# Row maxima of a causal attention as a stream of their own, and float32r score products in pairs of row halves

## The chip, the cores and the metric

The kernel runs on one core of a Trainium2 chip. The metric is device time in microseconds (us) for one execution; the number given is the median of several runs. Five engines of the core work side by side and wait for each other through semaphores: TensorE (PE in the profile; PEld is its weight load), VectorE (DVE), ScalarE (ACT), GpSimd (POOL) and SyncE (SP), which here only issues DMAs. TensorE writes its products to PSUM, eight banks of 128 partitions by 512 float32; everything else lies in SBUF or in DRAM.

## What is computed

The input `x` is 4 sequences of 1024 tokens with 256 features. After a layer norm, one branch is a causal attention with 16 heads of 16 features, the other a feed-forward chain of six blocks (256 to 1024 to 256, exact GELU), and the two are joined with a SiLU gate.

```python
def attention(x, w_qkv, w_out):
    q, k, v = split(x @ w_qkv)                       # (4, 1024, 16 heads, 16)
    scores = einsum('bqhd,bkhd->bhqk', q / 4, k)
    scores = where(causal_mask, scores, -1e10)
    attn = softmax(scores, axis=-1)
    return einsum('bhqk,bkhd->bqhd', attn, v).reshape(b, s, 256) @ w_out

def ffn(x, W1, B1, W2, B2, LN_G, LN_B):
    for i in range(6):
        h = gelu(x @ W1[i].T + B1[i])                # 1024 hidden, exact gelu
        x = h @ W2[i].T + B2[i] + x
        if i < 5:
            x = layernorm(x, LN_G[i], LN_B[i])
    return x

xn = layernorm(x)
out = x + attention(xn, w_qkv, w_out) * silu(ffn(xn, ...))
```

## The kernel before

Four stages follow each other, each a block with a program of its own for every engine, and a barrier between two.

**Projection** (`project`). The 4096 tokens come in 8 groups of 512 (`GROUPS`, `GT`). A group is normalised, transposed, split into a high float32r part and a low rest (`p_gth`, `p_gtl`) and multiplied with the weights, split in the same way: three products (high by high, high by low, low by high) stand for one of full precision. Queries and keys are split into three bfloat16 parts and stored in DRAM (`q_parts`, `k_parts`). The transposed input is kept in SBUF for all tokens (`xth`, `xtl`), and so are its rows (`xres`).

**Feed-forward** (`mlp`). A *slot* is one block applied to one group of 512 tokens; there are 48. A slot has 8 *chunks* of 128 hidden units. For chunk k TensorE does `up(k)` (line 752: six products of 512 columns into `m_h_ps`), then `down(k - 2)` (line 763: twelve products of 256 columns into `m_y_ps`). ACT computes the GELU twice (lines 626 and 628, in float32 and rounded to float32r), DVE takes the difference (line 687, `m_hidl`), and both parts feed `down`. Before each slot of the blocks after the first, eight transposes (line 785) make the transposed input anew. In each slot DVE also adds the residual (line 663), computes statistics (lines 694 and 704) and both halves of the layer norm (lines 711 and 722), and splits one piece of the next block's weights (lines 651 to 655). `sweep` runs the slots in hardware loops. In the last two slots the row maxima of attention group 0 are searched beside the chunks (`piece`, `piece_max`). The rows go to DRAM (`mlp_out`).

**Attention** (`attend`). A *group* is 4 heads of one sequence, 16 in all. A softmax needs the maximum of each row of scores. So the scores are computed twice: first with the queries on the partitions, in 38 *pieces* of up to 512 columns per group (`piece_products`, lines 114 and 117; the second one adds the causal mask as a product with the identity), of which DVE takes the maximum (`row_max`, line 129). The negated maxima, in three bfloat16 parts, are transposed, and become three rows more of the query stack (rows 96 to 98; the key stack has ones there). Then the scores are computed with the keys on the partitions (line 1153, 99 rows deep, `a_st_ps`), ACT takes the exponential (line 1003, `a_prob`), POOL clears what lies above the diagonal (line 977), and TensorE multiplies with the values, four heads side by side on 32 columns each of its array (line 1172, `a_o_ps`). The *stacks* `qs` and `ks` of a group hold the parts in 96 rows; SP loads them with 12 DMAs of 16 rows each (`load_stacks`, line 99), two groups ahead, into one of four buffers. TensorE's order within a group comes from a plan computed while the program is written: `pace` counts columns and puts the pieces of the next groups where, by the constants `DVE_COLUMN`, `ACT_COLUMN` and so on, their bank is free. ACT also copies the results (line 1014). At the end SP first issues four loads for the last stage (`load_pair`), then the store of the last group.

**Combination** (`combine`). Tile by tile of 128 tokens the attention output is divided by its row sums, multiplied with `w_out`, gated with SiLU, added to `x` and stored.

## Time and profile before

| | us |
|---|---|
| median of 3 runs | 1801.35 |
| the runs | 1800.85 to 1807.49 |
| span of the profiled execution | 1806.1 |
| TensorE busy, share of that span | 95% |
| DVE busy | 64% |
| ACT busy | 53% |
| POOL busy | 18% |

The span is that of one profiled execution, 4.75 us above the median. Its stages, by the times at which their first and last products stand in the trace: projection until 95.3 us, feed-forward from 106.4 to 1239.7 us, attention until 1719.8 us, combination from 1741.8 us to the end. A matmul's row in the trace lasts longer than the time it keeps the array, since products overlap; the distance from one start to the next is what a product costs. So a busy share near 100% says that TensorE had something in flight, not that it worked at its best.

### The profile page before, as it was taken

How to read it: one execution, taken by the hardware profiler on the slowest of the kernel's cores; microseconds unless marked ns; L12 is line 12 of the kernel's file. 1: busy time of each engine (PE TensorE's matmuls, PEld its weight loads, DVE VectorE, ACT ScalarE, POOL GpSimd, SP SyncE). 2: the span in 40 equal slices, each digit the busy share in tenths (PEclk: the TensorE clock that was granted, in tenths of full speed). 3: DMA queues.
4: the chain of work that ended last, by engine and by line, in shares of the span. 5: the costliest groups of instructions: out<-in, count | busy, mean ns of one | idle time of the engine just before them, and what ended most of it. 6: DMA issues, size and time to landing. Idle time of an engine off the chain costs nothing. (4 is left out here: it accounts for less than half of the span.)

```text
span 1806.1 us, 33624 instructions
## 1 busy us (share of the span) xinstructions
PE 1716.2 (95%) x11664; PEld 1312.9 (73%) x11664; DVE 1149.1 (64%) x2325; ACT 958.0 (53%) x1364; POOL 323.2 (18%) x317
## 2 busy tenths in 40 slices
PE   6979999999999999999999999997999989999947
PEld 5869999999999989999999998875444433444236
DVE  7846666666666656666666643366877866877326
ACT  5834555555555545555555554432666665666723
POOL 3511111111111111111111111110121211121214
PEclk9989999999999999999999999998999998999969
DMA  6940000000000000000000050003474754574113
GB/s 206 306 140 13 12 17 16 13 12 17 13 9 12 17 16 12 13 17 12 16 12 12 0 83 24 23 24 64 76 112 75 109 84 73 88 107 73 48 57 137
DMA packets 104427, 97.97 MB, mean 54 GB/s; under 512 B 26636, under 2 KB 88588, under 8 KB 104316
## 3 DMA queue, kind: packets, MB, share of 16 engines
q1 hardware_dynamic: 104256, 96.39, 23.9%
q8 instruction: 69, 1.13, 0.3%
q14 instruction: 42, 0.34, 0.1%
q10 hardware_dynamic: 60, 0.10, 0.0%
HBM read 62.15 MB, written 29.62 MB: 51 GB/s over the span
## 5 line engine op out<-in xcount | busy, mean ns | idle before, releaser
L626 ACT ACTIVATE m_hid<-m_h_ps,m_b1s 128x512 f32<-128x512 f32 x384 | 264.3, 688 | 571.0 <-PE m_h_ps L752 558.9
L687 DVE TENSOR_TENSOR m_hidl<-m_hid,m_hidh 128x512 fp32r<-128x512 f32 x384 | 307.4, 809 | 323.9 <-ACT m_hidh L628 322.8
L129 DVE TENSOR_REDUCE mx<-a_s_ps 128x1 f32<-128x512 f32 (+3 forms) x570 | 341.2, 656 | 91.3 <-PE a_s_ps L117 87.8
L1003 ACT ACTIVATE a_prob<-a_st_ps 128x1024 f32<-128x1024 f32 (+1 forms) x320 | 289.9, 938 | 168.5 <-PE a_st_ps L1153 123.0
L752 PE MATMUL m_h_ps<-xth,shared 128*128 (+1 forms) x768 | 269.8, 397 | 12.3 <-DVE shared L655 12.2
L763 PE MATMUL m_y_ps<-shared,m_hidh 128*128 128x256 f32 x1536 | 277.9, 281 | 0.0
L628 ACT ACTIVATE m_hidh<-m_h_ps,m_b1s 128x512 fp32r<-128x512 f32 x384 | 261.8, 682 | 0.0
L763 PEld LDWEIGHTS m_y_ps<-shared,m_hidh 128*128 128x128 f32 x1536 | 246.6, 189 | 12.0 <-DVE m_hidl L687 0.4
L602 POOL TENSOR_TENSOR y<-y,m_b2s 128x1024 f32<-128x1024 f32 x47 | 112.8, 2400 | 708.3 <-DVE y L663 708.3
L763 PE MATMUL m_y_ps<-m_w2h,m_hidh 128*128 128x256 f32 x768 | 217.9, 284 | 0.6 <-DVE m_hidl L687 0.3
L763 PE MATMUL m_y_ps<-shared,m_hidl 128*128 128x256 f32 x768 | 215.8, 281 | 0.0
L763 PE MATMUL m_y_ps<-m_w2h,m_hidl 128*128 128x256 f32 x768 | 215.5, 281 | 0.0
L763 PE MATMUL m_y_ps<-m_w2l,m_hidh 128*128 128x256 f32 x768 | 215.4, 280 | 0.0
L752 PEld LDWEIGHTS m_h_ps<-xth,shared 128*128 128x128 f32 x768 | 145.3, 189 | 39.9 <-DVE shared L655 12.9
L1172 PE MATMUL a_o_ps<-a_prob,a_va 128*32 128x512 f32 (+3 forms) x1536 | 165.9, 504 | 1.4 <-issue 1.3
L752 PE MATMUL m_h_ps<-xth,m_w1h 128*128 (+1 forms) x384 | 155.5, 405 | 2.5 <-issue 2.5
L752 PE MATMUL m_h_ps<-xtl,shared 128*128 (+1 forms) x384 | 152.0, 396 | 0.0
L752 PE MATMUL m_h_ps<-xtl,m_w1h 128*128 (+1 forms) x384 | 151.7, 395 | 0.0
L763 PEld LDWEIGHTS m_y_ps<-m_w2h,m_hidh 128*128 128x128 f32 x768 | 144.3, 188 | 8.9 <-issue 2.3
L763 PEld LDWEIGHTS m_y_ps<-m_w2l,m_hidh 128*128 128x128 f32 x768 | 146.6, 191 | 5.0
L752 PE MATMUL m_h_ps<-xth,m_w1l 128*128 (+1 forms) x384 | 150.1, 391 | 0.1
L977 POOL TENSOR_SCALAR_AFFINE_SELECT a_prob<-a_prob 128x512 f32<-128x512 f32 x128 | 81.5, 637 | 379.6 <-ACT a_prob L1003 379.0
(115 smaller groups left out, 2648.3 us busy)
## 6 DMA issues: line engine op xcount, KB each, us to landing
q_parts<-p_part SPq DMA_DIRECT2D x16, 384.0 KB, 3.5
k_parts<-p_part SPq DMA_DIRECT2D x16, 384.0 KB, 3.0
m_raw<-w1t SPq DMA_DIRECT2D x48, 128.0 KB, 2.2
m_raw<-w2t SPq DMA_DIRECT2D x48, 128.0 KB, 2.4
shared<-q_parts SPq DMA_DIRECT2D x48, 128.0 KB, 4.6
shared<-k_parts SPq DMA_DIRECT2D x48, 128.0 KB, 7.7
a_qs<-q_parts SPq DMA_DIRECT2D x48, 128.0 KB, 4.6
a_ks<-k_parts SPq DMA_DIRECT2D x48, 128.0 KB, 7.4
```

The costliest lines, as they stand in the source:

```text
L129: return nc.vector.reduce_max(mx[:, half, first:first + heads, qt], scores, AX_X)
L602: nc.gpsimd.tensor_tensor(y[yu][:], y[yu][:], b2s[epar][:].broadcast_to([P, TILES, DIM]), ALU.add).then_inc(b2_added, 1)
L626: nc.scalar.activation(hid[k % 2][:], h_ps[k % 2][:], ACT.Gelu, bias=b1s[s.par][:, k:k + 1])
L628: nc.scalar.activation(hidh[k % 4][:], h_ps[k % 2][:], ACT.Gelu, bias=b1s[s.par][:, k:k + 1]).then_inc(gelu_done, 1)
L687: nc.vector.tensor_tensor(hidl[k % 4][:], hid[k % 2][:], hidh[k % 4][:].bitcast(F32), ALU.subtract).then_inc(low_done, 1)
L752: i = nc.tensor.matmul(h_ps[k % 2][:], w[s.par][:, c, k * P:(k + 1) * P], x[:, c, tokens], start=(c == 0 and w is w1h and x is xth), stop= ...
L763: i = nc.tensor.matmul(y_ps[s.u][:, j, :], h[k % 4][:, j * P:(j + 1) * P], w[s.par][:, k, :], start=(k == 0 and j % 2 == 0 and h is hidh a ...
L977: nc.gpsimd.affine_select(out=diag, in_=diag, compare_op=ALU.is_ge, fill=0.0, base=0, pattern=[[0, HG], [1, P]], channel_multiplier=-1).th ...
L1003: nc.scalar.activation(prob[step % BUFS][:, j:j + heads, 0:hi - lo], unit_ps(unit), ACT.Exp).then_inc(exp_done, 1)
L1172: i = nc.tensor.matmul(o_ps[2 * HD * j:2 * HD * (j + 1), lo - BANK * half:BANK], va[u][:, kt, j, :], prob[step % BUFS][:, j, 0:hi - lo], s ...
```

## The change

The search for row maxima becomes a class of its own, `MaxSearch`, with a list of 336 *visits*: 20 pieces and one transposition for each of 16 groups. The first 209 visits, that is groups 0 to 9 but for the last transposition, lie in the feed-forward stage; 127 lie in the attention stage, over its first 14 groups, about one for each step of a group. A visit writes into one pair of banks, `s_ps`, and has to wait until DVE is through with the visit before.

Queries and keys are split into two float32r parts instead of three bfloat16 ones. A stack then has 48 rows (three products of parts by 16), or 50 with the two parts of the shift. Two heads lie on the rows 0 to 63 and two on 64 to 127 (`SIDE`), so that two products, one of each side, use different row halves of TensorE's array. This holds for the search (`pe_visit`) and for the scores. The causal mask of the search leaves TensorE: DVE adds it from SBUF and takes the maximum with one `tensor_tensor_reduce` for each head, on the pieces that touch the diagonal; the others are one reduction of 1024 columns. Stacks for attention have two buffers instead of four; those of the search have two more (`mq`, `mk`), and so each group's parts are loaded twice. The shifts go through DRAM (`shifts`).

In the feed-forward stage the rows stay in SBUF in place (`xres`), the transposed input is kept for two slots only, all 48 slots transpose, the scaling with the norm's weights goes to POOL, the normalisation to ACT, and `m_y_ps` has one buffer instead of two. The first block's weights are split during the projection. `xtl` and `mlp_out` are no longer stored. In attention a group has 10 steps and 18 exponentials, all of 1024 columns, instead of 12 steps and 20; DVE copies the results instead of ACT. All loops but those of `combine` are written out.

```diff
-PARTS = 3
-STACK = 6 * HD
+PARTS = 2
+STACK = 3 * HD
 ROWS = STACK + PARTS
...
+SIDE = P // 2
+PAIR = 2
+AHEAD = 10
...
+    def pe_visit(s, pe, s_ps, v):
...
+        for c in range(columns):
+            for side in range(2):
+                if c == 0 and v:
+                    pe.wait_ge(s.maxed, 2 * v - 1 + side)
+                rows = slice(SIDE * side, SIDE * side + STACK)
+                i = s.nc.tensor.matmul(s_ps[:, side, c * keys:(c + 1) * keys], s.q[m % 2][rows, first + c, qt * P:(qt + 1) * P],
+                                       s.k[m % 2][rows, first + c, half * BANK:half * BANK + keys], start=True, stop=True)
+        i.then_inc(s.done, 1)
...
+        if qt // HG != half:
+            s.nc.vector.reduce_max(mx[:, half, first::PAIR, qt], s_ps[:, :, 0:keys], AX_X).then_inc(s.maxed, 2)
+        else:
+            for side in range(2):
+                for c in range(columns):
+                    h = PAIR * side + first + c
+                    i = s.nc.vector.tensor_tensor_reduce(s.unused[:, v % 2, side, c * keys:(c + 1) * keys], s_ps[:, side, c * keys:(c + 1) * keys],
+                                                         s.causal[:, BANK - keys:BANK], 1.0, NEG, ALU.add, ALU.max, mx[:, half, h:h + 1, qt])
+                i.then_inc(s.maxed, 1)
...
+        for v in range(VISITS):
+            slot, place = divmod(2 * v, 9)
+            AT.setdefault(CH * (1 + slot) + (1, 4, 4, 5, 5, 6, 6, 7, 7)[place], []).append(v)
...
+            turn(0)
+            for n in range(CHUNKS + 2):
+                if n < CHUNKS:
+                    up(n)
+                if n % CH == 2 and n // CH + 1 < SLOTS:
+                    turn(n // CH + 1)
+                if n >= 2:
+                    down(n - 2)
+                for v in AT.get(n, ()):
+                    search.pe_visit(pe, s_ps, v)
...
+                    if n and n + 1 < N_GROUPS:
+                        sp.wait_ge(st_done, NU * n)
+                        load_stacks(sp, scratch, qs[(n + 1) % 2], ks[(n + 1) % 2], n + 1, keep["qk_loaded"][(n + 1) % 2])
+                        sp.wait_ge(search.stored, 16 * (n + 2))
+                        load_shift(sp, scratch, qs[(n + 1) % 2], n + 1, keep["qk_loaded"][(n + 1) % 2])
...
+            for at in range(ALL + LATE + 1):
+                n, step = divmod(at, NS)
+                if at < ALL:
+                    scores(n, FIRST_OF[step])
+                if 0 <= at - LATE < ALL:
+                    values(at - LATE)
+                if at < ALL and LAST_OF[step] > FIRST_OF[step]:
+                    scores(n, LAST_OF[step])
+                for v in AT.get(at, ()):
+                    search.pe_visit(pe, s_ps, v)
```

TensorE in the feed-forward stage, at the seam of two chunks. Before, `down` (line 763) is followed by `up` (line 752) directly:

```order
L763 MATMUL m_y_ps<-m_w2h,m_hidh 128x256
L763 MATMUL m_y_ps<-m_w2l,m_hidh 128x256
L763 MATMUL m_y_ps<-m_w2h,m_hidl 128x256
L749 REGISTER_ALU
L752 MATMUL m_h_ps<-xth,m_w1h 128x512
L752 MATMUL m_h_ps<-xtl,m_w1h 128x512
L752 MATMUL m_h_ps<-xth,m_w1l 128x512
```

Now, in four or five chunks of each slot, a pair of search products of line 164 stands between them (`mk`, `mq` are the search's stacks):

```order
L686 MATMUL m_y_ps<-w2h,m_hidh 128x256
L686 MATMUL m_y_ps<-w2l,m_hidh 128x256
L686 MATMUL m_y_ps<-w2h,m_hidl 128x256
L164 MATMUL m_s_ps<-mk,mq 128x512 x2
L673 MATMUL m_h_ps<-m_xth,w1h 128x512
L673 MATMUL m_h_ps<-m_xtl,w1h 128x512
L673 MATMUL m_h_ps<-m_xth,w1l 128x512
```

What moved in is a block of another shape of the array between two full ones.

TensorE in attention, before: pieces of the search (lines 114 and 117), scores (line 1153) and values (line 1172) in the plan's order.

```order
L1153 MATMUL a_st_ps<-shared 128x384
L1172 MATMUL a_o_ps<-a_prob,a_va 32x512 x4
L1151 REGISTER_ALU
L1153 MATMUL a_st_ps<-shared 128x384 x2
L1151 REGISTER_ALU
L1153 MATMUL a_st_ps<-shared 128x256 x4
L1165 REGISTER_ALU
L1172 MATMUL a_o_ps<-a_prob,a_va 32x512 x4
```

Now: scores are line 878, values line 897, the search line 164.

```order
L878 MATMUL a_st_ps<-shared 128x512 x2
L164 MATMUL a_s_ps<-mk,mq 128x512 x2
L878 MATMUL a_st_ps<-shared 128x512 x2
L897 MATMUL a_o_ps<-a_prob,va 32x512 x4
L878 MATMUL a_st_ps<-shared 128x512 x2
L164 MATMUL a_s_ps<-mk,mq 128x512 x2
```

A step has two pairs of scores, one block of values and one visit; the order no longer depends on a plan of when banks come free.

SP in attention, now: the loads of a group's stacks (line 86, `shared`) and shift (line 93), a search load (line 86, `mq` and `mk`) after the results' store, and then the next group's stacks.

```order
L782 DMA x_rows<-x 128x2x256
L86 DMA shared<-q_parts 16x2x1024 x6
L86 DMA shared<-k_parts 16x2x1024 x6
L93 DMA shared<-shifts 2x2048 x2
L105 DMA v_raw<-values 128x8x64
L775 DMA attention_t<-a_oout 17x1024 x4
L86 DMA mq<-q_parts 16x2x1024 x6
L86 DMA mk<-k_parts 16x2x1024 x6
L782 DMA x_rows<-x 128x2x256
L86 DMA shared<-q_parts 16x2x1024 x6
```

The stacks of group n + 1 are now loaded while group n runs; before they were loaded two groups ahead. The search loads, four in this stage, stand in the same queue.

## Rows read from the trace of the kernel before

**Rows 1.** Busy time by stretch: us, PE, PEld, DVE, ACT, POOL, PEclk, DMA share, GB/s

```profile
0.00:95.30 95.30, 79.43 (x448) 68.15 (x448) 71.46 (x146) 65.58 (x96) 45.51 (x50) 1.00 0.77 258
95.30:106.40 11.10, 0.02 (x1) 0.02 (x1) 1.26 (x4) 2.33 (x3) 1.62 (x2) 0.59 0.58 184
106.40:1239.70 1133.30, 1126.54 (x7312) 1015.84 (x7312) 681.78 (x1377) 561.54 (x848) 160.20 (x87) 1.00 0.08 19
1239.70:1257.50 17.80, 8.77 (x38) 4.28 (x39) 11.11 (x21) 1.30 (x2) 2.58 (x4) 0.62 0.57 110
1257.50:1719.80 462.30, 452.97 (x3483) 180.36 (x3481) 339.27 (x648) 302.93 (x352) 89.86 (x143) 0.98 0.51 85
1719.80:1741.80 22.00, 0.00 (x0) 0.00 (x0) 1.12 (x2) 2.10 (x3) 0.00 (x0) 0.55 0.11 39
1741.80:1806.10 64.30, 48.46 (x384) 44.23 (x384) 43.10 (x128) 22.21 (x64) 23.42 (x32) 0.87 0.34 118
```

**Rows 2.** Timeline of TensorE in feed-forward: start us, us, line, operation

```profile
158.01 1.03 PE L785 MATMUL m_tr_ps<-ident,y 128*128 128x128 f32 x8
158.80 0.48 PE L752 MATMUL m_h_ps<-xth,shared 128*128 x1
...
700.68 0.40 PE L752 MATMUL m_h_ps<-xth,m_w1h 128*128 128x512 f32 x1
...
702.07 0.28 PE L763 MATMUL m_y_ps<-m_w2h,m_hidh 128*128 128x256 f32 x1
...
703.48 0.40 PE L752 MATMUL m_h_ps<-xth,m_w1h 128*128 128x512 f32 x1
```

**Rows 3.** Timeline of TensorE in attention: scores, a block of values, search pieces

```profile
1361.20 0.38 PE L1153 MATMUL a_st_ps<-a_qs,a_ks 99*128 99x512 bf16 x1
1361.51 1.06 PE L1172 MATMUL a_o_ps<-a_prob,a_va 128*32 128x512 f32 x8
1362.51 0.28 PE L114 MATMUL a_s_ps<-shared 96*128 96x256 bf16 x1
...
1366.08 0.38 PE L114 MATMUL a_s_ps<-shared 96*128 96x512 bf16 x1
1366.30 0.22 PE L117 MATMUL a_s_ps<-maskb,identb 128*128 128x128 bf16 x1
1366.36 0.76 PE L1153 MATMUL a_st_ps<-a_qs,a_ks 99*128 99x512 bf16 x3
```

**Rows 4.** Groups by line and shape: count | busy us, mean ns | idle before, releaser

```profile
L687 DVE TENSOR_TENSOR m_hidl<-m_hid,m_hidh 128x512 fp32r<-128x512 f32 x384 | 307.4, 809 | 323.9 <-ACT m_hidh L628 322.8
L626 ACT ACTIVATE m_hid<-m_h_ps,m_b1s 128x512 f32<-128x512 f32 x384 | 264.3, 688 | 571.0 <-PE m_h_ps L752 558.9 <-issue 3.5 <-DVE m_hidl L687 1.9
L129 DVE TENSOR_REDUCE mx<-a_s_ps 128x1 f32<-128x512 f32 x360 | 224.4, 683 | 62.3 <-PE a_s_ps L117 58.8 <-PE a_s_ps L114 3.3
L663 DVE TENSOR_TENSOR y<-m_y_ps,xres 128x1024 f32<-128x1024 f32 x48 | 58.8, 1225 | 111.1 <-PE m_y_ps L763 111.1
L704 DVE BATCH_NORM_AGGREGATE m_mv<-m_stats 128x2 f32<-128x6 f32 x160 | 14.8, 155 | 0.0
```

**Rows 5.** Timeline of the last attention group, which has no search beside it

```profile
1710.49 1.07 PE L1172 MATMUL a_o_ps<-a_prob,a_va 128*32 128x512 f32 x8
...
1712.13 3.69 ACT L1003 ACTIVATE a_prob<-a_st_ps 128x1024 f32<-128x1024 f32 x4 [0.34 <-PE a_st_ps L1153]
1712.45 1.07 PE L1172 MATMUL a_o_ps<-a_prob,a_va 128*32 128x512 f32 x8
```

**Rows 6.** Busy time by stretch again: stack loads alone, and the projection's middle

```profile
1042.00:1066.00 24.00, 24.00 (x161) 21.93 (x160) 13.61 (x27) 12.02 (x18) 3.59 (x2) 1.00 0.91 126
...
45.00:90.00 45.00, 43.49 (x261) 37.58 (x260) 37.55 (x68) 37.57 (x56) 25.81 (x23) 1.00 0.91 305
```

**Rows 7.** Timeline of SP's DMA issues, for one stack and at attention's end

```profile
1339.34 2.78 SPq L99 DMA_DIRECT2D shared<-q_parts  x6
...
1706.39 14.00 SPq L1195 DMA_DIRECT2D ot<-attention_t  x4
```

More of the change, by code:

```diff
@@ L121, in by_head @@
-def by_head(bank, piece):
-    _, _, _, heads, keys = piece
-    return bank[:, 0:heads * keys].rearrange("p (h n) -> p h n", n=keys)
-def row_max(nc, mx, scores, piece):
-    qt, half, first, heads, _ = piece
-    return nc.vector.reduce_max(mx[:, half, first:first + heads, qt], scores, AX_X)
-def project(nc, x, wqkv, scratch, keep):
+            columns = min(BANK // keys, PAIR)
+            pieces += [(qt, half, c, columns, keys) for c in range(0, PAIR, columns)]
+    return pieces
+PIECES = max_pieces()
@@ L591, in _ @@
+            for n in range(2):
+                sp.wait_ge(keep["qk_loaded"][n], (LOADS + NM_LOADS) * 16)
+            sp.wait_ge(keep["ones_loaded"], 4 * 16)
         @block.gpsimd
         def _(pool):
[L593 to L598 removed]
@@ L637, in _, with high, normalise @@
-            sweep(act, slot, begin)
+            def high(t):
+                act.wait_ge(transposed, t + 1)
+                nc.scalar.activation(xth[t % 2][:], tr_ps[:], ACT.Copy).then_inc(xth_done, 1)
+            def normalise(t):
+                act.wait_ge(shift_ready, t + 1)
+                for j in range(TILES):
+                    row = xres[:, TILES * (t % GROUPS) + j, :]
+                    m = nc.scalar.activation(row, row, ACT.Identity, bias=shift[:, j:j + 1], scale=rstd[:, j:j + 1])
+                m.then_inc(normed, 1)
@@ new lines, with attend @@
+DIAGONALS = [[sum(hi - lo for _, lo, hi in parts[:i]) for i, (kt, _, _) in enumerate(parts) if kt // HG == half] for half, parts in STEPS]
+SELECTS = sum(len(d) for d in DIAGONALS)
+BUFS = 3
+LATE = 2
+def attend(nc, x, wout, scratch, keep, search):
+    od = scratch["o"]
+    ALL = NS * N_GROUPS
+    VISITS = range(search.at[AHEAD, 0], len(search.visits))
+    AT = {}
+    weights = [0.5 if WIDTH[step] < BANK else 1.0 for step in range(NS)]
+    total = sum(weights) * (N_GROUPS - 2)
+    for v in VISITS:
+        due = total * (v - VISITS[0]) / len(VISITS)
+        at = 0
+        while due >= weights[at % NS]:
+            due -= weights[at % NS]
+            at += 1
+        AT.setdefault(at, []).append(v)
+    STEP_OF = {v: at for at, visits in AT.items() for v in visits}
```

1349 lines of the change are left out of this document (549 added, 800 removed).

## The prediction, made blind

> **What bounds the kernel now.** I read the busy time by stretch first, cut at the seams of the stages [rows 1]. The feed-forward stage takes 1133.3 us and has TensorE busy for 1126.5 of them at the full granted clock; attention takes 462.3 us with TensorE busy for 453.0. DVE and ACT are busy for 60% and 50% of the first, 73% and 66% of the second. Then the timeline, because a busy TensorE may still be slow. In feed-forward one chunk goes from 700.68 to 703.48: 2.80 us, of which `up` takes 1.39 and `down` 1.41 [rows 2]. 384 chunks are 1075 us, nearly the whole stage, so nothing but TensorE's products bounds it. In attention a block of values of 512 columns keeps TensorE for 1.00 us (1361.51 to 1362.51), a search piece of 512 columns with its mask for 0.28 us, and a score product for about 0.22 us [rows 3]. Per group (sums over the 36 tiles of 128 by 128 of a head): search 22528 columns, 9.9 us at 0.28 us per 640; scores 18432 columns, 7.9 us; values nine times 512 columns, 9.0 us, and about 0.25 us for each of 12 blocks that the array needs to change its shape. That is near 29 us, and a group lasts 465 / 16 = 29 us. TensorE bounds attention too, by the search above all.
>
> **Feed-forward.** Chunks stay as they are: 1075 us. Transpositions: 47 beside the first, where there were 40, each 0.79 us plus about 0.08 for the late product behind it [rows 2]: 41 us. New are 209 visits. The trace has no product on half the rows. The stream of a visit is 461 columns on average per half (9216 by 20 pieces), 0.21 us at the pace of `up`, if both halves run side by side; 0.42 if they don't. Changing the shape: around a block of values TensorE loses 0.09 us ahead (1361.20 plus 0.22 against 1361.51) and 0.15 us behind (1.00 against 0.85, which four times 512 columns take at 2.4 GHz) [rows 3], 0.24 in all. For a visit I add 0.10 for the second half's weights, which in a lone pair have nothing to hide behind. So 0.55 us each, 115 us in all. Bounds: 0.31 (no change of shape to pay), 65 us; 0.87 (halves in sequence, and float32r weights of 0.19 us uncovered twice), 182 us. I take 0.55, since the block of values is the nearest row.
>
> Do the others keep up? A visit costs DVE 1.22 us where it is one reduction of 1024 columns (the residual's row has this size) [rows 4]. On the diagonal it is two to four passes of together 512 to 1024 columns plus a read-out for each; the trace has no such instruction. At 0.68 us per 512 [rows 4] and 0.15 for the read-out (the short instruction of line 704), a mean visit costs 1.42 us; if the operation needed two passes, 2.0. Per slot DVE then has 6.5 (eight times 0.81), 1.2 for the transposed rest, 1.3 for the residual, 2.2 for statistics, 1.4 for weights and 6.4 for visits: 19 of 25 us. A visit waits for DVE's maximum of the one before, a chunk earlier; DVE starts about 2.3 us behind `up` and ends by 3.9, TensorE comes back at 4.7. No stall, while DVE has 0.8 us to spare. ACT loses a copy and gains four small ones; its two GELUs of 0.69 us leave half the chunk free [rows 4]. POOL gets two passes more for each slot, behind which nothing of the chunk waits. Stage: 1075 + 41 + 115 + 2 for the cold start = 1233 us against 1133.
>
> **Projection and its seam.** TensorE's work is the same. A group's DMA grows from 3.0 to 3.3 MB; in the middle of the stage the queues moved 305 GB/s at a share of 0.91 [rows 6], so up to 5 us may come on top. I take 97 us, and 10 for the seam (barrier, then a transposition in place of the wait for the first weights): 107 against 106.4.
>
> **Seam to attention.** Before 17.8 us [rows 1]: store of the rows, barrier, and a serial chain from the maxima of group 0 to the first exponential. The first two groups' stacks and shifts now land before. Residual 1.3, POOL 2.4, barrier 3, exponentials' table and first scores 2.3: 9 us.
>
> **Attention.** A group is 18 exponentials of 1024 columns. Back to back they start every 0.92 us (3.69 for four, with the last one's full length) [rows 5], so ACT needs 16.6 us per group and a full step, two of them, 1.84 us. TensorE in a full step: two pairs of scores 0.47, a block of values 1.00 and the change of shape 0.10, a visit next to the scores 0.23: 1.80 us. Both are nearly equal, and both wait for each other through two pairs of banks. The last group before the change, free of search but with scores of 0.88, ran at 1.96 us per full step (1710.49 to 1712.45) [rows 5]. I take 2.0. In addition a visit returns to DVE once a step: product 0.4, two passes with read-out 1.7, and TensorE is back after 2.0, so diagonal visits cost a few tenths. 19.5 us per group with search (14), 18.3 without (2): 310 us. Then DMA. A stack is 1.5 MB; 24 loads of 3 MB took 24 us at 126 GB/s and a share of 0.91 [rows 6], so one stack takes 12 us behind 5.6 us of issue time, half of it exposed [rows 7]. From the start of group n to the arrival of stack and shift for n + 1 I count 15 us of 19.5: hidden. Four search loads of 12 us stand ahead of a following stack in the same queue; they leave the next one about 3 us late each: 12 us. Start and tail 3 us. Together 325 us against 462.3.
>
> **The rest.** The results' last store still follows four loads of 14 us at SP [rows 7]; 22 us of seam and 64 us of combination stay [rows 1].
>
> **Sum.** 107 + 1233 + 9 + 325 + 22 + 64 = 1760 us, against the span of 1806.1. The median is 0.9974 of that span, so 1755 us. Attention and its seam give 146 us, feed-forward takes back 100. It is a difference of two large numbers, and both hang on the price of a pair on row halves.
>
> **Rival 1, slower: the two row halves don't run side by side.** A pair of 512 columns then costs 0.46 instead of 0.23 us. Feed-forward: 209 times 0.21, 44 us more. Attention: a full step has 0.93 + 1.10 + 0.46 = 2.5 us of TensorE, 23.2 us per group with search, 18.7 without: 365 us, 40 more. Span 1844, time 1839. It decides from the point at which a pair costs over 0.36 us, where the 46 us gained are gone. Against it: values of four heads, eight products of 512 columns, take 1.00 us on column strips [rows 3]; one after the other, at 0.22 us each, they would take 1.76. For it: no row shows row halves. The Trainium skill (TensorE: Matmul & The Clock Gate, Part 3) gives a speedup of 3.07 for four row tiles instead of 4; by that rate a pair would cost 0.30 us, and the forecast would move up by about 26 us. No row here has row tiles.
>
> **Rival 2: stack loads bound attention.** Rows are now 4 KB at a distance of 32 KB in DRAM, where they were 2 KB at 24 KB. If the rate fell from 126 to 90 GB/s, a stack would take 17 us, the chain 20.7 us per group, and each search load 13 us: 379 us for attention, time 1809. For it: attention's queues are at a share of 0.51 before, at a group time of 29 us [rows 1], which is 15 us of a group and leaves little of 19. Against it: the mean does not show that larger rows are slower. The Trainium skill (DMA: Bandwidth & Descriptors, in its table of pitfalls) warns of row pitches at large powers of two, 207 GB/s at 512 KB and less from 2 MB on; that alone is above the 126 GB/s measured here, and would change nothing.
>
> **Rival 3: the small prices vanish.** If the change of shape hides (0.31 us per visit) and ACT runs at 0.92 us throughout (266 us plus 17 for start and DMA), feed-forward is 1183 and attention 283: span 1668, time 1664.
>
> **How the numbers follow.** Forecast 1755 us, chance 0.66; in it lie the dearer DVE pass (attention 28 us more) and the dearer stores (5). Rival 3 has 0.10, rival 2 0.09, rival 1 0.15. The main case by itself reaches from 1700 to 1800. The range for 8 in 10 is 1685 to 1812: it takes in rival 2 and leaves out rival 1 and most of rival 3. Faster by over 0.5% (which is about what a measurement of this kernel can tell from no change): 0.66, less 0.03 for its upper end, plus 0.10, plus 0.03 of rival 2, so 0.76. Within 0.5%: 0.07. Slower: 0.17.
>
> **What would show it.** In the changed profile: chunks without a visit still 2.80 us apart, those with one 3.35; starts of the two products of a pair under 0.15 us apart, and the next full product about 0.5 us behind. Attention of about 19 to 20 us per group, with ACT's idle time under 15% and released by scores. In rival 1 the second product of a pair starts 0.2 us behind the first and ACT waits for TensorE a quarter of the time; in rival 2 TensorE's longest waits, once a group, end with a DMA into the stacks. DVE below 80% in feed-forward. I am wrong at the root if chunks without a visit grow, since that would mean a wait on DVE or ACT which I count as hidden.

## The result and the profile after

The changed kernel takes 1851.6 us (median of 4 runs, 1850.5 to 1853.8) against 1802.3 in the same comparison: a ratio of 1.027 (95% interval 1.025 to 1.029). It is slower by 49 us, where I had forecast 1755 and a gain of 46. The profiled execution has a span of 1848.7 us. Its stages, cut at the same seams as [rows 1] (the columns are those of [rows 1]); the fifth stretch is attention up to its last values, the sixth the seam and the combination's start:

```profile
0.00:112.90 112.90, 86.34 (x448) 73.78 (x448) 67.44 (x178) 35.78 (x48) 10.57 (x20) 0.92 0.70 240
112.90:122.20 9.30, 2.12 (x11) 1.58 (x9) 1.23 (x1) 3.33 (x3) 0.00 (x0) 0.63 0.52 152
122.20:1395.00 1272.80, 1250.14 (x7777) 1076.68 (x7777) 887.65 (x1842) 607.03 (x975) 378.55 (x169) 0.99 0.17 29
1395.00:1399.90 4.90, 1.40 (x10) 1.19 (x8) 0.86 (x2) 1.28 (x1) 2.34 (x1) 0.87 0.14 16
1399.90:1763.90 364.00, 313.48 (x2595) 128.08 (x2593) 169.29 (x491) 276.73 (x288) 87.20 (x142) 0.91 0.70 116
1765.00:1787.00 22.00, 1.17 (x8) 0.97 (x8) 1.59 (x4) 2.01 (x3) 0.00 (x0) 0.55 0.09 34
```

Against the terms of the sum: projection and its seam 122.2 (forecast 107), feed-forward 1272.8 (1233), seam 4.9 (9), attention 364.0 (325), the rest 84.8 (86). The differences are 15, 40, -4, 39 and -1 and make up the 89 us between the forecast span of 1760 and 1848.7. In three stages TensorE is no longer busy all the time: it is idle for 27 us of the projection (16 before), 23 of feed-forward (7) and 51 of attention (9).

The pair on row halves is not the cause. Timeline of TensorE in feed-forward (columns as in [rows 2]); `m_s_ps` is a visit of twice 512 columns:

```profile
699.93 0.50 PE L164 MATMUL m_s_ps<-mk,mq 48*128 48x512 f32 x2
700.36 0.50 PE L673 MATMUL m_h_ps<-m_xth,shared 128*128 128x512 f32 x1
...
703.36 0.50 PE L164 MATMUL m_s_ps<-mk,mq 48*128 48x512 f32 x2
703.79 0.50 PE L673 MATMUL m_h_ps<-m_xth,shared 128*128 128x512 f32 x1
```

Both products of the pair together last 0.50 us and the next product starts 0.43 behind the first; the first full product then needs 0.10 more than usual before the next one. In the trace the two products of such a pair start 0.003 us apart (median of 120 pairs of 512 columns), which is the sign that the prediction asked for. The chunk lasts 3.43 us. One without a visit lasts 2.82, against the 2.80 of [rows 2]: 0.02 more in each of 384 chunks is 8 us, and no wait.

### The profile page after: what moved, and what is told of

Read it like the earlier page. It is cut to its first block and busy times, and to the rows that moved or that the text cites. A ratio compares the mean times of both kernels' runs of the same rounds, so it can differ in the third digit from the quotient of the medians.

```text
span 1848.7 us, 29436 instructions
## 1 busy us (share of the span) xinstructions
PE 1700.0 (92%) x11216; PEld 1323.2 (72%) x11216; DVE 1171.2 (63%) x2644; ACT 947.8 (51%) x1380; POOL 502.0 (27%) x364
## 5 line engine op out<-in xcount | busy, mean ns | idle before, releaser
L840 ACT ACTIVATE a_prob<-a_st_ps 128x1024 f32<-128x1024 f32 x288 | 276.7, 1025 | 84.9 <-PE a_st_ps L878 82.5
L673 PE MATMUL m_h_ps<-m_xth,shared 128*128 128x512 f32 x768 | 285.9, 413 | 11.7 <-issue 9.3
L686 PE MATMUL m_y_ps<-w2h,m_hidh 128*128 128x256 f32 x768 | 217.2, 283 | 0.0
L686 PE MATMUL m_y_ps<-w2l,m_hidh 128*128 128x256 f32 x768 | 214.6, 279 | 0.0
L686 PE MATMUL m_y_ps<-w2h,m_hidl 128*128 128x256 f32 x768 | 214.1, 279 | 0.0
L897 PE MATMUL a_o_ps<-a_prob,va 128*32 128x512 f32 (+3 forms) x1536 | 167.5, 526 | 43.0 <-POOL a_prob L821 43.0
L673 PE MATMUL m_h_ps<-m_xth,w1h 128*128 128x512 f32 x384 | 163.4, 426 | 13.4 <-issue 13.4
L673 PE MATMUL m_h_ps<-m_xtl,shared 128*128 128x512 f32 x384 | 153.1, 399 | 0.0
L673 PE MATMUL m_h_ps<-m_xth,w1l 128*128 128x512 f32 x384 | 152.9, 398 | 0.0
L673 PE MATMUL m_h_ps<-m_xtl,w1h 128*128 128x512 f32 x384 | 152.3, 397 | 0.0
```

What stands on the lines that cost most here:

```text
L673: m = nc.tensor.matmul(h_ps[n % 2][:], w[i % 2][:, c, k * P:(k + 1) * P], x[t % 2][:, c, :], start=(c == 0 and w is w1h and x is xth), sto ...
L686: m = nc.tensor.matmul(y_ps[:, j, :], h[n % 4][:, j * P:(j + 1) * P], w[par][:, k, :], start=(k == 0 and j % 2 == 0 and h is hidh and w is ...
L840: nc.scalar.activation(to, scores, ACT.Exp).then_inc(exp_done, 1)
L897: i = nc.tensor.matmul(o_ps[half][2 * HD * j:2 * HD * (j + 1), lo - BANK * half:hi - BANK * half], va[n % 2][:, kt, j, :], prob[at % BUFS] ...
```

## Experiments

Each kernel is the changed one with the edits shown, unless it says otherwise, and a gain is against its 1851.6 us. Ratios are to the kernel before, timed beside it.

### 1 and 2. Five waits in feed-forward

The waits of TensorE on weights in this stage (who waited for whom: total us, times, longest) and, below, the timeline of all engines at one of them, the end of a block:

```profile
PE m_h_ps L673 <- issue: 22.7, 5, 4.8
```

```profile
539.12 2.39 POOL L553 TENSOR_TENSOR xres<-xres,m_lng 128x1024 f32<-128x1024 f32 x1 [6.85 <-ACT xres L572]
...
540.52 1.54 DVE L636 TENSOR_TENSOR m_hidl<-m_hid,m_hidh 128x512 fp32r<-128x512 f32 x1 [1.49 <-ACT m_hidh L587]
541.59 2.67 POOL L555 TENSOR_TENSOR xres<-xres,m_lnb 128x1024 f32<-128x1024 f32 x1
541.98 2.42 DVE L218 CAST shared<-raw 128x256 fp32r<-128x256 f32 x1
...
545.50 0.77 PE L673 MATMUL m_h_ps<-m_xth,shared 128*128 128x512 f32 x1 [4.80 <-issue]
...
546.07 0.63 PE L673 MATMUL m_h_ps<-m_xtl,shared 128*128 128x512 f32 x1
...
546.49 0.63 PE L673 MATMUL m_h_ps<-m_xth,shared 128*128 128x512 f32 x1
```

The reader is to see three things. DVE's difference `m_hidl` takes 1.54 us instead of 0.69 and the cast 2.42 instead of 0.29, both while POOL's passes for gain and bias run; the second pass ends at 544.26 and the cast at 544.40. The last split of the block ends at 545.40, and only then may the first `up` of the next block run, 4.80 us late. And behind the wait products of 512 columns start at a distance of 0.42 us instead of 0.23 (546.07 and 546.49): the clock has fallen to the lower level, 1.2 GHz (the granted clock is 1.00 from 540 to 545 us and 0.66 from 545 to 550), and the wait is paid a second time in part.

Experiment 1 moves the split to chunk 2:

```diff
-                if k == 7 and t < LAST:
+                if k == 2 and t < LAST:
                     dve.wait_ge(raw_loaded[g % 2], 32 * (t // 2 + 1))
                     split_piece(nc, dve, keep, (i + 1) % 2, g, w_high, t + 1).then_inc(w_split, 1)
```

> The changed kernel with one edit: DVE splits the slot's weight piece at chunk 2 instead of chunk 7. In the changed kernel feed-forward lasts 1272.8 us, and TensorE is idle for 22.7 us of it in five waits of up to 4.8 us, one ahead of the first `up` of each new block, which waits for the last of the eight splits. At chunk 7 POOL's two passes of 2.4 and 2.7 us run, and DVE's casts of the weights take 2.4 us and 1.8 us where the same shape took 0.29 us in the projection. Theory A (DVE's casts are held up by POOL's passes, and the split, ready only at the edge of the block, comes too late): the five waits go, with them some 4 us of lower clock behind them; feed-forward 1246 us, time 1825 (ratio 0.986 to the changed kernel's 1851.6, 1.013 to the one before). The casts fall to about 0.3 us, unless POOL's first pass meets them. Theory B (the wait at the edge has another cause, say x_ready behind POOL's longer chain or the transposed input): the waits stay, 1850.

Measured: 1830.1 us, ratio to before 1.015 (1.013 to 1.017), a gain of 21.5. The five waits are gone and the casts take 0.27 us (median). One new wait of 8.5 us came in the first slot, where the raw weights land 13.9 us after DVE asks for them, behind the first search loads; without it the gain would have been 30, against the 27 forecast. Feed-forward takes 1251 us instead of 1273.

Experiment 2 leaves the split where it was and takes POOL's two passes away:

```diff
-                    nc.gpsimd.tensor_tensor(xx, xx, lng[i % 2][:].broadcast_to([P, TILES, DIM]), ALU.mult).then_inc(scaled, 1)
-                    pool.wait_ge(scaled, t + 1)
-                    nc.gpsimd.tensor_tensor(xx, xx, lnb[i % 2][:].broadcast_to([P, TILES, DIM]), ALU.add).then_inc(x_ready, 1)
+                    nc.gpsimd.memset(idle[:], 0.0).then_inc(x_ready, 1)
```

> The changed kernel without the layer norm's gain and bias: POOL's two passes per slot (2.4 and 2.7 us) are replaced by a memset of one column, and the split stays at chunk 7. Left out of the computation: the scaling by gain and the bias in the feed-forward chain. Theory A (POOL's passes hold up DVE): the cast of the first weight takes 0.3 us instead of 2.4, the difference `m_hidl` about 0.81 us instead of 0.90, and the five idle waits of TensorE (22.7 us) vanish although the split stays where it is; time near 1825. Rival (DVE is simply behind at chunk 7, because of its visits at chunks 4 to 7): casts 0.3 us, but the waits stay at 2 to 5 us each, time 1840 to 1850. Rival (the raw weights land late): casts stay long, 1850.

Measured: 1828.3 us in one run. The groups of DVE in feed-forward, the changed kernel first, then this one (columns as in [rows 4]):

```profile
L636 DVE TENSOR_TENSOR m_hidl<-m_hid,m_hidh 128x512 fp32r<-128x512 f32 x384 | 346.3, 902 | 351.2 <-ACT m_hidh L587 350.4
L218 DVE CAST w1h<-raw 128x256 fp32r<-128x256 f32 x24 | 57.7, 2405 | 0.0
```

```profile
L635 DVE TENSOR_TENSOR m_hidl<-m_hid,m_hidh 128x512 fp32r<-128x512 f32 x384 | 283.9, 739 | 414.6 <-ACT m_hidh L586 414.4
L218 DVE CAST w1h<-raw 128x256 fp32r<-128x256 f32 x24 | 6.8, 285 | 0.6 <-DMA raw<-w2t 0.6
```

The cast falls from 2405 to 285 ns and the difference from 902 to 739, although nothing of DVE's own work was changed: POOL's passes hold up the cast and the difference, which read and write SBUF alone. The changed kernel's trace says so directly, too. 39 of its 40 first casts of this stage run beside the pass for the bias, take 2.5 us and end 0.15 us behind it (medians). The difference takes 0.69 us in 299 cases without a pass beside it and 1.55 in the 40 beside the pass for the gain (medians). What is left above 0.69 in the 739 comes from a third pass of POOL (line 546), which this run keeps. That agrees with the Trainium skill (SBUF — State Buffer, Who interferes with whom, with the rule it rests on in "SBUF: two separate sides"), by which a GpSimd instruction and a DVE instruction in a two-port mode, or one with two SBUF inputs if GpSimd's reads SBUF as well, exclude each other for their whole length. It also agrees that the reductions, which read PSUM, take 1.22 us, the ten wholly beside a pass of POOL as well as the other 70. Of the waits 7.8 us remained (five, up to 1.8), so the rival has a part: DVE is late at chunk 7 without these two passes, too.

### 3. The input's place in SP's queue

In the projection DVE waits 27.9 us, in 6 waits, for the group's input, since its load stands behind the stores of four parts, the values and two weight pieces.

```diff
-                if g + 2 < GROUPS:
-                    sp.wait_ge(normed, g + 1)
-                    load_x(g + 2)
+                if g == 0:
+                    sp.wait_ge(normed, 1)
+                    load_x(2)
                 for m in range(4):
+                    if m == 2 and g + 3 < GROUPS:
+                        sp.wait_ge(normed, g + 2)
+                        load_x(g + 3)
                     sp.wait_ge(part1_done, 4 * g + m + 1)
```

> The changed kernel with one edit in the projection: SP issues the load of a group's input one group earlier, between the query and the key stores, instead of behind the stores, the values and two weight pieces. In the changed kernel DVE waits 27.9 us in 6 waits for this input, and the stage ends at 112.9 us instead of 95.3. Theory A (the place in SP's queue): these waits go, the stage ends at 100 us or before, time 1839. Theory B (bytes: each group moves 3.3 MB instead of 3.0, and the queues' rate bounds the stage): input comes earlier but stores and weight pieces later; the stage ends at 110 or later, time 1848 to 1852.

Measured: 1829.8 us, ratio 1.015 (1.013 to 1.017), a gain of 21.8, more than theory A asked for. The middle of the stage (columns as in [rows 6]), the changed kernel first, then this one:

```profile
20.00:80.00 60.00, 49.76 (x272) 42.75 (x271) 36.73 (x102) 21.61 (x29) 5.03 (x5) 0.91 0.73 245
```

```profile
20.00:80.00 60.00, 60.00 (x364) 53.25 (x364) 51.31 (x137) 29.52 (x40) 6.05 (x6) 1.00 0.98 343
```

TensorE is busy throughout, at the full clock, and the queues move 343 GB/s at a share of 0.98. The first `up` starts at 99.7 us instead of 122.2, and 22 of these 22.5 us reach the end. So bytes did not limit the stage; they come close to it now.

### 4 to 7. The loads of the attention stage

In attention these waits of the changed kernel are the longest but for those of idle engines (waited for: total us, times, longest):

```profile
POOL va L111 <- DMA v_raw<-values: 139.3, 12, 18.8
...
ACT a_prob L840 <- PE a_st_ps L878: 82.5, 82, 12.1
...
PE a_o_ps L897 <- POOL a_prob L821: 43.0, 12, 10.4
```

and one group of them, from the timelines of SP, POOL and TensorE, in this order:

```profile
1470.47 0.38 SPq L105 DMA_DIRECT2D v_raw<-values  x1
1470.90 13.21 SPq L775 DMA_DIRECT2D attention_t<-a_oout  x4
```

```profile
1485.86 0.61 POOL L111 COPY va<-v_raw 128x512 f32<-128x512 f32 x1 [18.08 <-DMA v_raw<-values]
1486.42 1.22 POOL L821 TENSOR_SCALAR_AFFINE_SELECT a_prob<-a_prob 128x512 f32<-128x512 f32 x2
```

```profile
1487.11 1.93 PE L897 MATMUL a_o_ps<-a_prob,va 128*32 128x512 f32 x8 [9.34 <-POOL a_prob L821]
```

The values' load is issued at 1470.47 behind the stack and lands 15 us later. POOL waits for it in front of a mask, TensorE's values wait for the mask, and the scores of the next steps stand behind these values. The block then takes 1.93 us instead of 1.07, at the lower clock (the granted clock of the stage is 0.91, and 0.98 before). Such waits are not spread evenly. From the first exponential of one group to that of the next there are 19.0 to 22.6 us in the other groups, but 29.7, 28.2, 30.6 and 26.1 in the four (3, 5, 7 and 9) around whose start a search load stands in SP's queue.

The obvious edit is to issue the values first:

```diff
                     if n and n + 1 < N_GROUPS:
+                        sp.wait_ge(keep["v_ready"], n)
+                        load_values(sp, scratch, keep, n + 1)
                         sp.wait_ge(st_done, NU * n)
...
-                        sp.wait_ge(keep["v_ready"], n)
-                        load_values(sp, scratch, keep, n + 1)
```

> The changed kernel with one edit: SP issues the load of the next group's values (256 KB) ahead of the twelve stack loads instead of behind them. In the changed kernel POOL waits 139.3 us in 12 waits for these values, with its masks queued behind, and TensorE's values wait for the masks (92.6 us in 40 waits); attention takes 365.1 us. Theory A (the order of the loads is the cause): POOL's waits go, attention falls to the 325 us of the prediction, time 1812. Theory B (the stacks themselves, at 120 to 140 GB/s, arrive no sooner than the values did; POOL's wait only shows it first): the wait moves to TensorE's first scores of a group, which then wait for a DMA into the stacks; attention 355 to 362, time 1842 to 1849.

Measured: 1884.0 us, ratio 1.045 (1.044 to 1.047), a loss of 32. Theory A fell, and B did not give the size. Its waits and one of SP's rows:

```profile
POOL va L111 <- DMA v_raw<-values: 117.0, 13, 13.6
...
PE a_st_ps L878 <- DMA shared<-shifts: 33.9, 12, 9.2
```

```profile
1483.80 12.04 SPq L86 DMA_DIRECT2D shared<-q_parts  x6
```

SP now needs 8 to 12 us to issue six stack loads, for which it needs 2.65 with a free queue. What stood ahead of them are the result's four stores and two loads of 256 KB. So something in the queue is slow, and every order only chooses who stands behind it. Two candidates: the stack loads, each on 16 partitions, and the stores, each on 17.

The stacks first. In DRAM the two parts of a feature are neighbours, so that two of the three row sets, interleaved row by row, are one load of 32 partitions (for the keys the low part is stored first, which makes the pairs high by low and low by high):

```diff
+            both = src[first:first + PAIR * HD, :, SEQ * bt:SEQ * (bt + 1)].rearrange("(c d) a n -> (d a) c n", d=HD)
+            sp.dma_start(to[SIDE * side:SIDE * side + PARTS * HD, :, :].bitcast(F32), both).then_inc(loaded, 16)
+            rows = src[first:first + PAIR * HD, high, SEQ * bt:SEQ * (bt + 1)].rearrange("(c d) n -> d c n", d=HD)
+            sp.dma_start(to[SIDE * side + PARTS * HD:SIDE * side + STACK, :, :].bitcast(F32), rows).then_inc(loaded, 16)
```

> The changed kernel with the stack loads (those of attention and of the search) in eight DMAs instead of twelve: two of the three row sets of a side are interleaved row by row and come as one DMA of 32 partitions, the third as one of 16; the same bytes, the same three products of parts. In the changed kernel 24 or more loads of 16 partitions in flight moved 120 to 141 GB/s at a DMA share of 0.66 to 0.93 in attention. Theory A (16 destination partitions limit the rate, and a late stack, with the values behind it, holds attention): two thirds of the bytes move at a higher rate, a stack lands some 4 us earlier, attention falls from 365 to 340 us or below, time 1827. Theory B (the queue is held up by other transfers, such as the stores of 17 partitions): rate as before, time 1845 to 1852.

Measured: 1829.9 us, ratio 1.015 (1.014 to 1.017), a gain of 21.7. Attention takes 342 us. The edit also makes eight DMAs of twelve, and no run separates that from their width. Then the stores, and with them the last stage's loads:

```diff
-                for j in range(HG):
-                    sp.dma_start(od[hg, j, :, SEQ * bt:SEQ * (bt + 1)],
-                                 oout[n % 2][2 * HD * j:2 * HD * j + HD + 1, :]).then_inc(o_stored[n % 2], 16)
+                sp.dma_start(od[hg, :, :, SEQ * bt:SEQ * (bt + 1)].rearrange("j r n -> (j r) n"), oout[n % 2][:]).then_inc(o_stored[n % 2], 16)
...
-            "ot": [b.sb(f"ot{c}", [HG * (HD + 1), HG, 2 * P]) for c in range(OT)],
+            "ot": [b.sb(f"ot{c}", [P, HG, 2 * P]) for c in range(OT)],
```

> The changed kernel with each group's result stored as one DMA of 128 partitions (512 KB, of which 15 of 32 rows per head repeat the row sum) instead of four DMAs of 17 partitions (272 KB), and with the last stage's loads of 128 instead of 68 partitions. In the changed kernel SP needs 5.5 to 14 us to issue a group's four stores, and 16.9 us for four loads of 68 partitions. Theory A (a DMA of 17 rows is not spread over the 16 DMA engines, and what is queued behind it waits for the one that works): the issue of the stores falls below 1 us although more bytes move, stacks and values land earlier, attention 335 to 350 us, the seam to the last stage 12 instead of 21 us, time 1815 to 1830. Theory B (bytes bound attention): 0.24 MB more per group, attention 375, time 1855 or more. The last stage's transpositions of 128 rows instead of 68 cost TensorE about 5 us there in either case.

Measured: 1799.7 us, a ratio of 1.000 (0.998 to 1.001): a gain of 52, with 7.9 MB more to move. Attention of this kernel:

```profile
1399.90:1735.50 335.60, 305.90 (x2594) 125.35 (x2593) 170.66 (x492) 276.52 (x289) 87.74 (x142) 0.95 0.83 142
```

The queues move 142 GB/s instead of 116. Behind attention, from the last values to the first transposition of the combination, there are 5 us instead of 22, and the combination takes 55 instead of 63; I had expected it to grow by 5. This seam shows the stores by themselves, since nothing else is in flight at its end. The changed kernel first, then this one (columns as in [rows 1]):

```profile
1773.00:1783.00 10.00, 0.00 (x0) 0.00 (x0) 0.00 (x0) 0.00 (x0) 0.00 (x0) 0.50 0.06 26
```

```profile
1736.00:1738.00 2.00, 0.00 (x0) 0.00 (x0) 0.00 (x0) 0.00 (x0) 0.00 (x0) 0.66 0.65 262
```

A share of 0.06 is one engine of 16. The packets in the trace say it exactly: the 68 rows of the last four stores go out one after the other, each in 0.16 us, from 1772.8 to 1783.4. The 128 rows of the single store take 0.16 us each as well, but all are through in 1.6 us. The edit changes the last stage's loads together with the stores; attention, where only the stores differ but for its end, gained 29 us. The same stores in four pieces tell whether the number of DMAs or their partitions matter:

```diff
-                sp.dma_start(od[hg, :, :, SEQ * bt:SEQ * (bt + 1)].rearrange("j r n -> (j r) n"), oout[n % 2][:]).then_inc(o_stored[n % 2], 16)
+                for j in range(HG):
+                    sp.dma_start(od[hg, j, :, SEQ * bt:SEQ * (bt + 1)], oout[n % 2][2 * HD * j:2 * HD * (j + 1), :]).then_inc(o_stored[n % 2], 16)
```

> The changed kernel with the results stored in four DMAs of 32 partitions per group (the same bytes as one DMA of 128), and the last stage's loads of 128 partitions as in the earlier edit. Storing a group in one DMA of 128 partitions instead of four of 17 gave 52 us in all, 29 of them in attention. Theory A (a DMA of 17 partitions is slow because its rows are not spread over the DMA engines): 32 partitions are spread, so the issue of the four takes about 2 us, attention 335 to 340 us, time 1797 to 1805. Theory B (the number of DMAs in SP's queue is what counts): the issue stays at 5 us or more, attention 350 to 365, time 1815 to 1830.

Measured: 1797.4 us, ratio 0.997 (0.996 to 0.999). Four DMAs of 32 partitions are as good as one of 128; the issue takes 1.7 or 5.0 us in the two groups that I read, so that number was too low, but attention is at 336 us. It was the 17 partitions, and not the number of DMAs. The Trainium skill (DMA: Bandwidth & Descriptors, Why a DMA increments its semaphore by 16 and not by 1) says how: a DMA is dealt to as many of the 16 engines as divide the sizes of its slowest dimensions on both sides, which gives one engine for 17 rows, four for 68 and 16 for 32 or 128. The traces agree: a share of 0.06 for 17 rows, 0.26 for 68 (from 1766 to 1768 us, when the last stage's loads run), and 0.65 for 128.

### 8. The edits together

The split at chunk 2 (but for the first slot), the input earlier in SP's queue, wide stacks and wide results:

> The changed kernel with four edits at once: the weight split at chunk 2 (in the first slot still at chunk 7, since its raw weights land 13.9 us late there), the projection's input loaded a group earlier, the stacks in DMAs of 32 and 16 partitions, the results in DMAs of 128. If the causes are what I hold them to be and independent, the gains add: feed-forward 1246 us, projection and seam 104, attention 325 or less, the seam behind it 12 us: span about 1245 + 104 + 325 + 5 + 12 + 65 = 1757, time 1755 to 1765. If attention is bound by ACT and TensorE together rather than by loads, it stays near 345 and the time near 1780. If loads bound it in bytes, 1800.

Measured: 1725.1 us, ratio 0.958 (0.956 to 0.959), below everything that was expected. Its stages:

```profile
0.00:91.70 91.70, 77.75 (x448) 68.44 (x448) 67.45 (x178) 35.87 (x48) 10.60 (x20) 1.00 0.84 295
91.70:101.00 9.30, 2.14 (x11) 1.56 (x10) 1.23 (x1) 3.33 (x3) 0.00 (x0) 0.78 0.56 156
101.00:1342.00 1241.00, 1241.00 (x7777) 1069.70 (x7777) 798.34 (x1842) 608.32 (x975) 377.90 (x169) 1.00 0.15 29
1342.00:1347.00 5.00, 1.50 (x11) 1.08 (x9) 0.95 (x2) 1.29 (x2) 2.34 (x1) 0.91 0.03 4
1347.00:1664.90 317.90, 302.17 (x2591) 124.08 (x2591) 170.35 (x492) 276.26 (x288) 88.46 (x142) 0.97 0.76 149
1664.90:1670.20 5.30, 0.00 (x0) 0.00 (x0) 1.79 (x3) 1.47 (x2) 0.00 (x0) 0.50 0.25 99
1670.20:1725.40 55.20, 48.19 (x384) 45.41 (x384) 43.28 (x128) 22.30 (x64) 23.57 (x32) 0.96 0.66 191
```

The first `up` came 3 us sooner than in that sum, feed-forward is 5 us shorter, attention 7, the seam behind it 7 and the combination 10. In feed-forward TensorE is never idle. The 200 chunks with a visit take 3.37 us in the mean and those without one 2.82 (median), so a visit costs 0.55 us. Adding the values' load ahead of the stacks to this kernel:

> The four edits together, plus the values' load ahead of the stack loads, the edit that by itself cost 32 us. In it SP needed 8 to 12 us for the first stack loads of a group and TensorE waited for the stacks. Theory A (that loss came from the stores of 17 partitions, which stood just ahead of the stacks in a full queue): with results of 128 partitions the loss is gone; POOL's waits for the values, still 80 us in 12 waits, go, and the time is 1715 to 1725, against 1725.1. Theory B (any load ahead of the stacks delays them by its own time, and the stacks are the tighter of the two): attention longer by 1 to 2 us per group, time 1735 to 1755.

Measured: 1720.7 us, ratio 0.955 (0.953 to 0.957). The edit that cost 32 us in the slow queue gains 4 in the free one, as theory A says. This is the fastest kernel, 81 us below the one before the change and 131 below the changed one.

### 9. The price of a second stream

Both products of a visit read the rows 0 to 47, which is the rival in which row halves take turns, made true:

```diff
-                rows = slice(SIDE * side, SIDE * side + STACK)
+                rows = slice(0, STACK)
```

> The changed kernel, where the search takes both products of a pair from the rows 0 to 47 instead of one from each row half. Changed in the computation: the maxima of two of four heads are those of the other two, so the shift of the softmax is not the row's own maximum. Theory A (row halves run side by side): a visit in feed-forward grows by the stream of its second product, 461 columns, 0.21 us: 209 times that is 44 us on feed-forward (1272.8 to 1317), and some 10 to 25 us on attention. Theory B (the halves took turns anyway, and the 0.61 us of a visit are two streams and a short change of shape): no change.

Measured: 1909.5 us in one run, 58 more. Feed-forward takes 1311.5 us, 39 more, or 0.19 us for each visit; attention takes 385, 21 more. The two products now start 0.34 us apart instead of 0.003 and the next full one 0.66 behind the first instead of 0.43. Row halves do run side by side. Of the 0.55 us of a visit 0.19 to 0.21 are the stream, and the other 0.35 stand where the shape changes.

### 10. The same repair on the kernel before

> The kernel before the change with one edit: each group's result stored as one DMA of 128 partitions instead of four of 17, and the last stage's loads of 128 partitions instead of 68. In the changed kernel this edit gave 52 us: 29 in attention, 16 at the seam behind it, 8 in the combination. Theory A (in the kernel before, attention is bound by TensorE, and its queues have slack): attention stays at 462 us, seam and combination give 20 to 25 us, time 1778 to 1782, ratio about 0.988. Theory B (the loads held attention before, too): 10 us or more of attention besides, time 1770 or less.

Measured: 1775.1 us, ratio 0.985 (0.984 to 0.987), a gain of 27 on the kernel before. Its attention takes 456 us instead of 462.3, the seam 5 instead of 22, the combination 56 instead of 64. Attention, seam and combination of the two traces give 31 us where the medians give 27, so the 6 of attention are hardly more than the spread. The slow stores were in both kernels; before, a group of 29 us left the queues time (SP issued the four in 2.9 us), and in a group of 20 us they did not fit. With its stores repaired the kernel before takes 1775.1 us, and the changed one with all its repairs 1720.7. That is not quite the worth of the change, since the stacks of the kernel before still come in narrow loads, and no run widened them there.

### 11 and 12. How much search belongs into which stage

With `AHEAD = 9` instead of 10 in the kernel of section 8:

> The four edits together, with 9 instead of 10 groups searched inside feed-forward: 21 visits and one pair of stack loads move to the attention stage. With 10 groups feed-forward lasts 1241 us, of which a visit costs 0.59 us, and attention 318 us. If a visit in attention hides between the exponentials (scores beside it have its shape already), feed-forward gives 12 us and attention takes back 2 to 5 us: 1716 to 1720. If loads or TensorE bound attention, it takes back 12 us or more: 1725 or later.

Measured: 1778.2 us (ratio 0.985, 0.982 to 0.989), a loss of 53 for 21 visits moved. Feed-forward gave the 12 us, attention took 384 us. Waits of TensorE in it, and its timeline behind one (columns as above):

```profile
PE a_s_ps L164 <- DVE x_mx L180: 11.6, 11, 1.4
PE a_s_ps L164 <- DVE x_mx L185: 8.5, 13, 0.9
```

```profile
1513.22 0.69 PE L164 MATMUL a_s_ps<-mk,mq 48*128 48x384 f32 x2 [1.39 <-DVE x_mx L180]
1513.70 0.63 PE L880 MATMUL a_st_ps<-shared 50*128 50x512 f32 x2
1514.26 1.93 PE L899 MATMUL a_o_ps<-a_prob,va 128*32 128x384 f32 x16
```

There are 148 visits for 140 steps, and the rule that places them gives two to 20 of the steps (to one with `AHEAD = 10`). A visit directly behind another waits for DVE's maximum of the first, 22 times, up to 1.4 us and 20 us in all. The blocks behind the wait shown run at the lower clock: 1.93 us instead of 1.07 in the same form. The granted clock of the stage is 0.88 instead of 0.97. The waits are 20 us, the loss in attention 66. What the lower clock can cost at most is the missing share of the stage: 0.12 of 384 us against 0.03 of 318, some 36 us more. That is an estimate from the two traces, and no run separated it; a fifth search load and longer waits on POOL (14 us against 8) came with the edit as well.

The other way, without any search in attention:

> The four edits together, without the search in the attention stage: its 127 visits, their loads and stores are left out, and groups 9 to 15 use the shift of group 8. The prediction put a group at 19.5 us with search and 18.3 without, and ACT alone needs 16.6 us per group. With search, attention lasts 317.9 us. If ACT and TensorE's values bound the stage, it falls to about 290 (16 times 18.0); if the stack loads of the attention groups themselves bound it, it stays above 305.

Measured: 1714.1 us in one run; attention takes 305.4 us, 12.5 less. I had put 290 and 305 as the two sides, and it lies on the edge. A group without search lasts 18.7 us, from the second group on without exception, against a forecast of 18.3, and the 127 visits cost 0.1 us each there.

## Why the prediction was wrong

**What bounds the kernel**: right for before. **The price of a visit in feed-forward**: 0.55 us, as forecast, of which the stream is 0.19 (forecast 0.21) and the change of shape with the second half's weights 0.35 (0.34). That the sum of estimates from another shape met it so closely is in part luck. The repaired stage is 8 us above the forecast because each chunk takes 2.82 us instead of 2.80.

**"Do the others keep up?"** is the first step that failed. It added DVE's instructions at their durations of before, and said of POOL's two new passes that nothing of the chunk waits behind them. They take DVE's time in another way: the cast that took 0.29 us took 2.4, and POOL's passes reach TensorE through it. Together with the place of the split, one chunk ahead of its use, this cost 32 of the 40 us (1272.8 against 1241). The sum of 19 of 25 us for a slot was about right in total (DVE was busy for 18.5, what POOL held up included), and it was no use, because the wait arises in one chunk of eight, in five of the 48 slots.

**Projection**: I forecast 97 us and up to 5 more for bytes. The bytes never bound. The step that failed is one that I didn't take: the load of the input had moved behind two weight pieces in SP's order. With the load moved ahead, the first `up` starts at 99.7 us, 7 before the 107 of the sum; where it was, at 122.2.

**Seam to attention**: 4.9 against 9. **Attention by its engines**: 19.5 us per group and 310 for all; the repaired kernels took 318 and 314, with the four collisions among them, and most of their groups take 19.1. The pair of engines was right.

**"15 us of 19.5: hidden"** is the step that cost the other 39 us. It took a stack's rate (126 GB/s, [rows 6]) from a stretch without stores, and let the stores follow at no price, though [rows 7] show that four loads on 68 partitions take 14 us to issue: the one row in which a DMA of few partitions was seen to be slow. Widened, the stores alone gave back 29 us of attention. Besides, I counted only to the arrival of stack and shift, and not to that of the values behind them, for which POOL waits ahead of the masks that TensorE's values need. The term that shows it is that of the four search loads, "about 3 us late each: 12 us". Their four groups take 115 us together where four times 19.5 are 78, so this term measured 37 us, 25 of the 39. With the stores repaired it is 5. Rival 2 named the right resource, priced at 379 us where 364 came; its mechanism, the pitch of the rows in DRAM, is not what the runs showed: the repaired kernels load rows at the same pitch, and their attention takes 318 and 314. Its sign, TensorE's longest waits ending with a DMA into the stacks, did not appear either; they end with POOL's mask.

**Rival 1** is refuted: made true, it costs 58 us. **Rival 3** did not come; ACT's pace of 16.6 us a group was never reached.

**The range** ended at 1812 and left out 1852. Of the three misses, 15, 40 and 39 us, all but the 8 us of the longer chunks are waits, on things that I had called hidden or had not looked at. They add, and my range counted only on one of them at a time.

## What to carry to other kernels

When a stage is made faster by a third, everything that was hidden in its old length has to be priced again at its own rate, each transfer in the order of its queue, and the slowest form of transfer first: stores of 17 partitions held up everything behind them, and of 32 they didn't. When work is moved to GpSimd, look for the instructions of DVE that work from SBUF to SBUF at the same moment, and keep those on which TensorE waits away from them. A wait of TensorE can cost more than its length. Behind the nine waits of 4.5 to 10.4 us in the changed kernel's feed-forward and attention the products run at half the clock; behind the five of 1.2 to 1.8 us in its attention they don't; with `AHEAD = 9` they do behind six of the eight waits of 1.4 us. So look at the granted clock behind a wait before pricing it.

## What was not expected of the hardware

- A cast of 128 by 256 on DVE, 0.29 us alone, takes 2.4 us beside a `tensor_tensor` of 128 by 1024 on GpSimd, and ends 0.15 us behind it; reductions from PSUM keep their 1.22 us beside one.
- The same results stored from 17 partitions at a time or from 32: 28 us in a stage of 364, although the second form moves 88% more bytes. The rows of the first form leave one after the other, 0.16 us each.
- Two thirds of a stack's rows loaded to 32 partitions at a time instead of 16: attention 22 us shorter.
- Two float32r products on different row halves of TensorE share one stream's time: 0.43 us for twice 512 columns with the change of shape, 0.66 where they share rows.
- A stage with 22 waits of up to 1.4 us more, 20 us in all, was 66 us longer, at a granted clock of 0.88 instead of 0.97.
